# Two outer rings of the mixture stages made deeper: 12 gathered and 12 result tiles in place of 8 and 3

## The reference

```python
# layer 1: one expert a token (argmax of the router's logits)
h = gelu(einsum('bsh,hi->bsi', x + 0.1 * game_emb[e], w1[e]) + b1[e])
y = einsum('bsi,ih->bsh', h, w2[e]) + b2[e]
# layer 2: two experts a token, their outputs weighed by the router
h = gelu(einsum('td,edh->teh', xf, w1))
y = einsum('teh,ehd->ted', h, w2)
out = einsum('te,ted->td', cw, y)
```

## Time and profile before

| | us |
|---|---|
| median of three runs | 1891.1 |
| lowest and highest run | 1890.85 and 1893.7 |
| span of the profiled execution | 1895.7 |
| GpSimd busy in it | 367.1 |
| TensorE busy in it | 1516.1 |
| VectorE busy in it | 1055.2 |
| ScalarE busy in it | 939.8 |

### The profile page before, as it was taken

One profiled execution on the slowest core, in us unless ns is written; L12 is line 12 of the kernel. 1 busy time (PEld: TensorE's weight loads), 2 busy tenths in 40 slices (PEclk: granted clock), 3 DMA queues, 4 the chain that ended last, 5 costly groups with the idle time before them and its releaser, 6 DMA issues. The chain is left out here.

```text
span 1895.7 us, 27344 instructions
## 1 busy us (share of the span) xinstructions
PE 1516.1 (80%) x9044; PEld 827.3 (44%) x9102; DVE 1055.2 (56%) x2297; ACT 939.8 (50%) x2171; POOL 367.1 (19%) x512
## 2 busy tenths in 40 slices
PE   4895757999999586775599898987577885988879
PEld 4454653555555375665222222222477552222245
DVE  6576331333334524312788988894611575788656
ACT  3454334444444334112387787875311434777733
POOL 1230530000000163564030101000266101101000
PEclk7796877999999788798699999998688896999989
DMA  2002434120200343544320303000444304223000
GB/s 71 5 1 86 142 92 122 26 67 1 67 1 1 110 141 111 188 128 120 86 79 1 78 1 96 1 1 1 140 131 120 98 6 113 64 60 79 1 1 22
DMA packets 96180, 126.09 MB, mean 67 GB/s; under 512 B 14336, under 2 KB 65408, under 8 KB 95664
## 3 DMA queue, kind: packets, MB, share of 16 engines
q1 hardware_dynamic: 86384, 105.23, 19.3%
q0 software_dynamic: 7936, 16.27, 3.2%
q10 hardware_dynamic: 1728, 2.88, 0.7%
HBM read 87.54 MB, written 36.80 MB: 66 GB/s over the span
## 5 line engine op out<-in xcount | busy, mean ns | idle before, releaser
L2119 DVE TENSOR_REDUCE MAXI<-psum 128x2 f32<-128x1024 f32 x384 | 457.2, 1220 | 90.4 <-PE psum L1926 88.6
L2036 ACT ACTIVATE EX<-psum 128x512 f32<-128x512 f32 x768 | 412.8, 606 | 107.0 <-PE psum L1947 106.9
L1947 PE MATMUL psum<-QM,KM 64*128 64x512 bf16 x768 | 227.4, 383 | 32.3 <-ACT EX L2036 21.4
L2420 PE MATMUL psum<-EX,N 128*128 128x512 f32 x512 | 238.0, 608 | 0.0
L2482 ACT ACTIVATE EX<-psum 128x512 f32<-128x512 f32 x256 | 149.2, 598 | 173.7 <-PE psum L2412 173.7
L1926 PE MATMUL psum<-KM,QS 64*128 64x512 bf16 x768 | 184.5, 401 | 35.3 <-DVE MAXI L2119 14.9
L1957 PE MATMUL psum<-EX,VST 128*32 128x512 f32 x1536 | 203.1, 604 | 1.0 <-ACT OT L2050 1.0
L1382 DVE TENSOR_SCALAR m_Y<-psum 128x128 f32<-128x128 f32 x124 | 36.0, 290 | 280.6 <-PE psum L1165 159.9
L1165 PE MATMUL psum<-m_DOWN,m_H 128*128 x992 | 148.6, 298 | 48.0 <-issue 30.9
L1151 PE MATMUL psum<-m_XT,m_W 128*128 128x128 f32 x992 | 154.4, 306 | 18.8 <-DVE m_XT L1375 13.7
L1165 PEld LDWEIGHTS psum<-m_DOWN,m_H 128*128 128x128 f32 x992 | 135.6, 212 | 53.5 <-issue 53.2
(11 more groups left out here) (330 smaller groups left out, 2020.7 us busy)
## 6 DMA issues: line engine op xcount, KB each, us to landing
m_W<-in_w_dram SPq DMA_DIRECT2D x124, 256.0 KB
parts<-PART SPq DMA_DIRECT2D x24, 384.0 KB, 2.6
m_DOWN<-in_w_dram SPq DMA_DIRECT2D x32, 256.0 KB, 4.8
parts<-PART SPq DMA_DIRECT2D x24, 256.0 KB, 2.4
rows<-N SPq DMA_DIRECT2D x16, 256.0 KB, 3.1
N<-y SPq DMA_DIRECT2D x16, 256.0 KB, 4.0
QS<-parts SPq DMA_DIRECT2D x32, 128.0 KB, 3.7
QS<-parts SPq DMA_DIRECT2D x16, 256.0 KB, 5.9
```

The source lines that it names most:

```text
L1947: pe.matmul(bank_of(("score", n, i)), KM[r, buf, g, m, kt * P:(kt + 1) * P], QM[r, n % 2, MAPS[at] // slots, :], start=True, stop=True).th ...
L2036: act.activation(EX[:, n % 2, kt, MAPS[j], :], bank_of(("score", n, i)), ACT.Exp, scale=SM_SCALE).then_inc(S["exp"].sem, 1)
L2119: dve.tensor_reduce(MAXI[:, n % 2, qt, columns], pair(i), AX, ALU.max, negate=True).then_inc(S["reduced"].sem, 1)
L2420: last = pe.matmul(banks[4 + j], N[:, n // per_b * TB + kt, :], EX[:, n % 2, kt, j, :], start=kt == 0, stop=kt == TB - 1)
```

## The change

`AHEAD` goes from 8 to 12, and the ring of result tiles `Y` from 3 tiles to `YS` = 12. The semaphores no longer follow the tiles: gathers share six (`IN_FLIGHT`) and scatters four (`OUT_FLIGHT`), and since two DMAs in flight may not count on one semaphore, a gather now also waits for gather r - 6 to have landed, and a scatter for scatter r - 4. VectorE's result waits for the scatter of slot r - 12. The final waits are for four counters in place of three.

```diff
-        AHEAD, DEEP = 8, 5
+        AHEAD, DEEP, YS = 12, 5, 12
+        IN_FLIGHT, OUT_FLIGHT = 6, 4
...
-        Y = sb("Y", [P, 3, P])
+        Y = sb("Y", [P, YS, P])
...
                 def gather(r):
                     if r >= AHEAD:
                         pool.wait_ge(S["turned"].sem, S["turned"].at(r - AHEAD + 1))
+                    if r >= IN_FLIGHT:
+                        pool.wait_ge(gathered[r % IN_FLIGHT].sem, gathered[r % IN_FLIGHT].at(16 * (r // IN_FLIGHT)))
...
                 def scatter(r):
                     pool.wait_ge(S["y"].sem, S["y"].at(r + 1))
+                    if r >= OUT_FLIGHT:
+                        pool.wait_ge(scattered[r % OUT_FLIGHT].sem, scattered[r % OUT_FLIGHT].at(16 * (r // OUT_FLIGHT)))
...
-                    if r >= 3:
-                        dve.wait_ge(scattered[r % 3].sem, scattered[r % 3].at(16 * (r // 3)))
-                    dve.tensor_scalar(Y[:, r % 3, :], banks[4 + r % 2][:, 0:P], 0.5 if one else 1.0, None, ALU.mult
+                    if r >= YS:
+                        before = r - YS
+                        dve.wait_ge(scattered[before % OUT_FLIGHT].sem,
+                                    scattered[before % OUT_FLIGHT].at(16 * (before // OUT_FLIGHT + 1)))
+                    dve.tensor_scalar(Y[:, r % YS, :], banks[4 + r % 2][:, 0:P], 0.5 if one else 1.0, None, ALU.mult
```

More of the change, by code:

```diff
@@ L1062, in moe @@
         resident = self.semaphore_of("moe_resident")
-        gathered = [self.semaphore_of(f"moe_gathered{i}") for i in range(AHEAD)]
-        scattered = [self.semaphore_of(f"moe_scattered{i}") for i in range(3)]
+        gathered = [self.semaphore_of(f"moe_gathered{i}") for i in range(IN_FLIGHT)]
+        scattered = [self.semaphore_of(f"moe_scattered{i}") for i in range(OUT_FLIGHT)]
         weights = [self.semaphore_of(f"moe_weights{i}") for i in range(DEEP)]
@@ L1096, in _ @@
                                  ).then_inc(weights[r % DEEP].sem, 16)
-                for i in range(3):
-                    sp.wait_ge(scattered[i].sem, scattered[i].at(16 * len(range(i, R, 3))))
+                for i in range(OUT_FLIGHT):
+                    sp.wait_ge(scattered[i].sem, scattered[i].at(16 * len(range(i, R, OUT_FLIGHT))))
                 for b in range(B):
@@ L1116, in gather @@
                         pool.wait_ge(S["turned"].sem, S["turned"].at(r - AHEAD + 1))
+                    if r >= IN_FLIGHT:
+                        pool.wait_ge(gathered[r % IN_FLIGHT].sem, gathered[r % IN_FLIGHT].at(16 * (r // IN_FLIGHT)))
                     pool.indirect_dma_start(XG[:, r % AHEAD, :], None, rows_dram,
                                             bass.IndirectOffsetOnAxis(ap=ROWS[:, 0, r:r + 1].bitcast(U32), axis=0)
-                                            ).then_inc(gathered[r % AHEAD].sem, 16)
+                                            ).then_inc(gathered[r % IN_FLIGHT].sem, 16)
                 def scatter(r):
                     pool.wait_ge(S["y"].sem, S["y"].at(r + 1))
+                    if r >= OUT_FLIGHT:
+                        pool.wait_ge(scattered[r % OUT_FLIGHT].sem, scattered[r % OUT_FLIGHT].at(16 * (r // OUT_FLIGHT)))
                     pool.indirect_dma_start(y_dram, bass.IndirectOffsetOnAxis(ap=ROWS[:, 1, r:r + 1].bitcast(U32), axis=0),
-                                            Y[:, r % 3, :], None).then_inc(scattered[r % 3].sem, 16)
+                                            Y[:, r % YS, :], None).then_inc(scattered[r % OUT_FLIGHT].sem, 16)
                 if fix_now:
@@ L1139, in turn @@
                 def turn(r):
-                    pe.wait_ge(gathered[r % AHEAD].sem, gathered[r % AHEAD].at(16 * (r // AHEAD + 1)))
+                    pe.wait_ge(gathered[r % IN_FLIGHT].sem, gathered[r % IN_FLIGHT].at(16 * (r // IN_FLIGHT + 1)))
                     if r >= 2:
@@ L1214, in _ @@
                     unread(3, 12)
-                    for i in range(3):
-                        pe.wait_ge(scattered[i].sem, scattered[i].at(16 * len(range(i, R, 3))))
+                    for i in range(OUT_FLIGHT):
+                        pe.wait_ge(scattered[i].sem, scattered[i].at(16 * len(range(i, R, OUT_FLIGHT))))
                     unread(3, 10)
@@ L1437, in moe @@
         resident.passed(16 * E)
[L1438 to L1441, removed]
+        for i in range(IN_FLIGHT):
+            gathered[i].passed(16 * len(range(i, R, IN_FLIGHT)))
+        for i in range(OUT_FLIGHT):
+            scattered[i].passed(16 * len(range(i, R, OUT_FLIGHT)))
         for i in range(DEEP):
```

## The result

| | before | changed |
|---|---|---|
| median, nine runs each, us | 1890.8 | 1896.9 |
| lowest and highest run, us | 1887.57 and 1893.7 | 1889.93 and 1898.57 |
| span of the profiled execution, us | 1895.7 | 1888.1 |

The ratio is 1.0029, with an interval of 1.0017 to 1.0041: the change makes the kernel slower by 3 to 8 us, where 7.5 us less was forecast. A run takes its span and 1.8 us. The two profiled executions stand the wrong way round: the one of before, 1895.7 + 1.8 us, is longer than any of its nine runs, and the one of the changed kernel is its fastest run. So stages are compared here, not spans, and with profiles of both kernels from one chip where there are some.

What follows compares the result with a forecast made beforehand. GpSimd's transfers were taken to bound the middle by making TensorE's completions visible late. Tail -19.7 us plus start +12.2 us, new waits 0, gave -7.5 us: 1891.1 to 1883.6 us, range 1868 to 1897.

Steps and rivals of the forecast that it cites:

- The bottleneck: Middle of each mixture: while transfers flow, TensorE's completions are seen late (4.8 us), and GpSimd waits for the result it held up.
- The rings were not full: Gathered and result rings in the middle rhythm: neither is full, so deepening them takes out no wait there by itself.
- The new waits: 184 second waits on gathers and scatters in the four mixtures: taken as 0, at most 5.5 us.
- The tail: End of each mixture: four more slots run without gathers, saving 5.1 us in two mixtures, 4.7 in two, 19.7 in all.
- The start: Ahead of each mixture's first scatter: four more gathers delay it by 3.05 us, 12.2 us in all, bounds 0 and 20.
- rival (b): GpSimd's stream sets all; each mixture's start gives back 5.0 us, -19.7 + 20 = 0, so 1891 us; chance 0.22.
- Rival (c): Middle and starts slower: rows of ten transfers, TensorE a row later, second waits show; +15 us at worst, about 1900; chance 0.15.
- last sign, lateness on scatters alone: In the longer tail: the forecast would be wrong as a whole if TensorE's completions were late on scatters alone; no size given.

Runs made afterwards that it cites:

- pause kernel: The changed kernel with three memsets (about 3.5 us) on GpSimd between the eighth and ninth of the twelve gathers ahead; one run, 1898.4 us.
- results ring alone: The kernel before with only the result ring 12 deep and scatters on four counters, eight gathers ahead; ratio 1.0009.
- gathers alone: The kernel before with only the gathered ring 12 deep and gathers on six counters, result ring of 3; ratio 1.0016.
- the kernel with the scatters last: The kernel before with a result ring as deep as the mixture's slots, all scatters behind the last gather; ratios 1.0198 and, on another chip, 1.0156.

## Why the prediction was wrong, step by step

**The bottleneck: right.** GpSimd's own row of transfers delays the result for which it then waits. The pause kernel shows it directly.

**The rings were not full: right.** The results ring alone moves nothing, and gathers alone have all of the change's effect on the stages.

**The new waits: right as far as it can be seen**: 0 was taken, and apart they measure 1.0001, within 3 us to either side.

**The tail: right in sum.** Predicted -19.7 us; middle and tail together gained 21.1 us on one chip and 21.6 on another. By mixtures it lay otherwise: 4.4 and 3.5 us where 5.1 were taken for those of 39 slots, since the tail's pace is 1.90 to 2.0 us, and the 1.79 came from five slots that included the short last ones (all eight of that tail give (887.01 - 871.48) / 8 = 1.94); 6.4 and 6.9 us where 4.7 were taken for those of 23. There the 1.9 us a slot was wrong as well, with 2.3 and 2.4 in the profile before and 1.9 and 2.3 in its repeat, and the middle's pace differed between the two kernels. That the sum fits owes something to luck: in the first pair of profiles the gain was 26.8.

**The start: here it failed.** The step is "12.2 us", put together from the first scatter going out at once behind the twelfth gather, so that the 2.42 us which it waited behind the eighth would be used up. The product was ready by then, that was right (773.82). But of the 2.42 us only the first 0.75 was time TensorE needed. The rest is the delay behind the end of a row and the result's own way to GpSimd, and that isn't used up by a longer row: it stands behind twelve gathers as well and is a little longer there, 2.84 us in all. So the four gathers cost their full 5.0 us and a bit, 5.6 in each mixture, 22.4 in all. That is 2.4 us over the upper bound (20) and is the prediction's rival (b), whose sign, a first scatter 17 us behind the first gather, came true. The prediction had the fact for it in hand, "2.3 us after GpSimd issued the last gather of the six", used it for the middle, and did not put it to the start. With 22.4 in place of 12.2 the sum is +2.7 us, and the loops measured +1.2 and +0.9 in the two pairs from one chip.

**Rival (c)** didn't come: rows stayed at six transfers, and the middle at 3.0 to 3.2 us a slot. The prediction's last sign, lateness on scatters alone, is true of the chip (the kernel with the scatters last) but not of this change: in most of its tail there are 0.8 us or more between the scatters.

**What stays open.** The runs put the change at +3.6 to +6 us, the loops at about +1. The other 3 us or so stay open. Nothing points to the second waits, and single profiles can't place them: the time outside the loops varied from 1501.5 to 1510.5 us from one to the next, in kernels that are the same there. So the start explains why no gain came, with 22.4 us in place of 12.2; it does not explain the whole loss.

## What to carry to other kernels

A wait that keeps ending a short time behind another engine's last instruction may be tied to that engine, and then moving work ahead of it moves the wait along; ask of each idle stretch whether it would be used up or only shifted before counting on it. Lengthening the prologue of a ring pays only for what the prologue can hide: here eight gathers ended just before TensorE's first product came (9.8 and 10.6 us after the first gather), four starved TensorE, and each one beyond eight was paid for in full. And where a difference is a fifth of a per cent, compare stages of several profiles, never two spans.

## What the runs showed of the hardware

On four of the five chips of the experiments, and not on the fifth, the other engines see TensorE's completions late while GpSimd issues indirect DMAs of 128 rows with 0.30 us between them: by 7 us in the start of the changed kernel, and with results as much as 24 us apart in a row of thirty scatters. In the start of the changed kernel's third mixture the transposes and the first product up to 771.3, 7.5 us into the row, were taken at once, and none from then to its end; in the longest rows one to three results get through. A break of about 2 us behind a row of six to twelve lets them through, and so do transfers 0.93 us apart; behind a row of 40 it took 6.4 us. ScalarE's and VectorE's completions are not held: TensorE took them within 0.13 us in the midst of the row of scatters. For this kernel it is worth some 64 us of 1890, by the estimate above.

The Trainium skill, "TensorE: Matmul & The Clock Gate", section "The cost: per-tile semaphore tail", puts increments behind matmuls at about 26 ns each. Behind a break the traces agree as far as they can tell: the changed kernel's product that ends at 780.12 + 2.07 = 782.19 is taken at 782.23, behind the row. For the product before it, which ended in the row, they don't: 7.1 us. Why a row of GpSimd's transfers does this, and what differs between the chips, no run here shows.
